# Second attention over whole 128-row blocks, with value rows placed by matmul and half-array score matmuls, in a one-core decoder layer

## The reference

```python
def proj(x, w):
    return (x @ w.T).reshape(B, -1, H, dk).transpose(0, 2, 1, 3)
Q, K, V = (proj(q, w_q), proj(k, w_k), proj(v, w_v))
scores = jnp.einsum('bhqd,bhkd->bhqk', Q, K) / jnp.sqrt(jnp.float32(dk))
scores = jnp.where(mask == 0, NEG, scores)
attn = jax.nn.softmax(scores, axis=-1)
out = jnp.einsum('bhqk,bhkd->bhqd', attn, V)
out = out.transpose(0, 2, 1, 3).reshape(B, S, D)
return out @ w_o.T
```

## Time and profile before

| | us |
|---|---|
| median of 3 runs | 1519.68 (1519.27 to 1520.58) |
| profiled execution | 1522.42 |
| its span | 1520.6 |
| PE busy | 1343.9 (88%) |
| DVE busy | 1113.7 (73%) |
| ACT busy | 925.7 (61%) |
| POOL busy | 730.0 (48%) |

### The profile page before, as it was taken

How to read it: one execution, slowest core, us unless ns; L and a number is a source line. 1 busy time by engine, 2 the same in 40 slices (tenths; PEclk the granted TensorE clock), 3 DMA queues, 4 the chain that set the end, 5 groups by cost and what they waited for, 6 DMA issues and landing times. The chain is left out here.

```text
span 1520.6 us, 48478 instructions
## 1 busy us (share of the span) xinstructions
PE 1343.9 (88%) x17429; PEld 1126.0 (74%) x17429; DVE 1113.7 (73%) x3110; ACT 925.7 (61%) x2255; POOL 730.0 (48%) x923
## 2 busy tenths in 40 slices
PE   3599989999999999999999999873899999999940
PEld 2478878888888888888888888641588888888820
DVE  4588878888888888888888889748455555555537
ACT  3566768777777777877777766623344444444426
POOL 3144564575575566566656644520244334444336
PEclk9799999999999999999999999995899999999975
DMA  9667666766757666666676664109532263323235
GB/s 219 127 155 162 164 149 164 143 137 179 143 132 186 138 143 162 155 145 143 167 146 135 156 112 88 26 15 411 165 79 74 77 157 98 76 77 76 74 134 208
DMA packets 293219, 209.01 MB, mean 137 GB/s; under 512 B 218782, under 2 KB 250654, under 8 KB 290560
## 3 DMA queue, kind: packets, MB, share of 16 engines
q1 hardware_dynamic: 281952, 184.01, 51.3%
q0 software_dynamic: 6816, 17.71, 3.9%
q10 hardware_dynamic: 4224, 4.19, 0.8%
HBM read 93.79 MB, written 65.93 MB: 105 GB/s over the span
## 5 line engine op out<-in xcount | busy, mean ns | idle before, releaser
L1635 PE MATMUL ps_e<-xt,wres 128*128 128x128 f16 x3408 | 343.4, 220 | 5.6 <-DMA xt<-xg 4.8
L1635 PEld LDWEIGHTS ps_e<-xt,wres 128*128 x3408 | 285.5, 98 | 77.6 <-issue 6.2
L1699 ACT ACTIVATE act_g<-ps_e,b 128x128 f32<-128x128 f32 x568 | 162.7, 369 | 207.8 <-PE ps_e L1635 207.6
L1642 PE MATMUL ps_e<-wres,g_hi 128*128 x568 | 214.5, 379 | 0.8 <-DVE g_lo L1722 0.8
L707 ACT ACTIVATE probs<-st_k,nmax 128x128 f32<-128x128 f32 (+1 forms) x512 | 199.6, 447 | 2.0 <-DVE nmax L914 1.9
L914 DVE CUSTOM_DVE_ANT_0 st_k<-ps,causal 128x128 f32<-128x128 f32 (+1 forms) x512 | 160.5, 351 | 35.6 <-PE ps L432 35.6
L1602 POOL DMA_INDIRECT z_scr<-e_y,dst_i x71 | 85.9, 1209 | 209.4 <-DVE e_y L1713 207.6
L714 ACT ACTIVATE pt_hi<-ps 128x384 f16<-128x384 f32 x256 | 125.0, 488 | 54.1 <-PE ps L440 31.8
L1644 PE MATMUL ps_e<-wres,g_lo 128*128 x568 | 154.8, 273 | 0.0
L1180 POOL TENSOR_TENSOR o_st<-o_norm,o_st 128x256 f16<-128x256 f32 x128 | 86.2, 673 | 133.6 <-ACT o_st L722 130.8
L1710 DVE SCALAR_TENSOR_TENSOR e_y<-ps_e,b 128x256 f32<-128x256 f32 x71 | 30.1, 424 | 158.9 <-PE ps_e L1644 158.9
(11 more groups left out here) (270 smaller groups left out, 4240.7 us busy)
## 6 DMA issues: line engine op xcount, KB each, us to landing
k_pair<-k_pair SPq DMA_DIRECT2D x96, 256.0 KB, 6.4
st_p<-in_moe_w SPq DMA_DIRECT2D x24, 768.0 KB, 6.2
w_scr<-st_p SPq DMA_DIRECT2D x24, 768.0 KB, 4.4
wres<-w_scr SPq DMA_DIRECT2D x18, 1024.0 KB, 21.6
v_scr<-v_tok SPq DMA_DIRECT2D x32, 512.0 KB, 3.8
v_pos<-v_scr SPq DMA_DIRECT2D x64, 256.0 KB, 6.2
q_st<-st_q SPq DMA_DIRECT2D x64, 128.0 KB, 3.4
z_scr<-zero SPq DMA_DIRECT2D x32, 256.0 KB, 3.6
```

The source lines that it names most:

```text
L1635: last = mm(out, w(c * FF + f * P, b, P), xt[:, t % X_BUFS, a, c], start=(m == 0), stop=(m == 5))
L1642: mm(out[:, 0:2 * D], g_hi[:, t % G_BUFS, f], w(KC * FF + f * D, 0, 2 * D), start=(f == 0), stop=False, skip_group_check=True)
L1699: nc.scalar.activation(act_g[:, k % 2, f], ps[:, 3 + 2 * (k % 2) + f // 4, (f % 4) * P:(f % 4 + 1) * P], ACT.Gelu, bias=bias[:, f:f + 1], ...
```

## The change

The 8 heads x 77 = 616 probabilities of a half are padded to 640 = 5 blocks of 128 (CHUNKS2) and are transposed and multiplied block by block, across the borders of heads. A block touches 2 or 3 heads; the 12 pairs of a block and a head are HEAD_SLOTS.

- Transposes: five of 128 x 128 in place of eight of 77. ACT and DVE write the parts from 128 x 384 and 128 x 256 in place of 77 x 512 twice.
- Values: for each block three matmuls over 128 rows with 34 or 51 columns (15 in place of 24). They need the values laid out by block rows with zeros outside each head (v2_own). In odd s, PE copies value rows to their block rows with a 0/1 matrix key_rows (value_rows, five matmuls for each cc), ACT brings them from PSUM to v2_rows (408 columns), and POOL multiplies by the 0/1 matrix slot_heads (own_values, 408 elements).
- Scores: k2_bd holds 4 heads. Heads 0 to 3 use rows 0 to 63 of the array and heads 4 to 7 rows 64 to 127, in alternation on two banks, six matmuls of 64 rows as before of 128. spread_k2 is half as wide.
- New waits: PE's value_rows waits for v2's low part, in the first pair for POOL's constants, and in its second half for ACT's first copy; x1's transposes wait for the second copy; pv2 waits for own_values. ACT's copy of the next values waits for value_rows.
- value_constants on POOL at the start of step 1 makes key_rows, slot_heads and the padding. head_rows is made in four selects in place of two.
- In the last norm a constant of 4 columns gives way to a broadcast of one.

The core of the diff:

```diff
@@ stage_c on PE
-                for j, bank in enumerate(banks2(t, cc)):
-                    out = bank[:, 0:4 * CTX]
-                    for m, (a, b) in enumerate(((q2_hi, 0), (q2_lo, 0), (q2_hi, 1))):
-                        last = mm(out, a[:, cc], k2_bd[:, b, cc, 4 * j:4 * j + 4].rearrange("p h k -> p (h k)"), start=(m == 0), stop=(m == 2))
+                for m, (a, b) in enumerate(((q2_hi, 0), (q2_lo, 0), (q2_hi, 1))):
+                    for j, bank in enumerate(banks2(t, cc)):
+                        rows = slice(j * P // 2, (j + 1) * P // 2)
+                        last = mm(bank[:, 0:4 * CTX], a[rows, cc], k2_bd[rows, b, cc].rearrange("p h k -> p (h k)"), start=(m == 0), stop=(m == 2))
...
-                    for n in range(4):
-                        last = nc.tensor.transpose(bank[0:CTX, n * P:(n + 1) * P], probs2_of(t, cc)[:, 4 * j + n], ident[:])
+                    for n, c in enumerate(BANK_CHUNKS[j]):
+                        last = nc.tensor.transpose(bank[:, n * P:(n + 1) * P], probs2_of(t, cc)[:, c * P:(c + 1) * P], ident[:])
@@ PE
+        def value_rows(t, cc):
+            if t % 2:
+                return
+            b = half(t)
+            if cc == 0:
+                pe.wait_ge(s_kv2_lo, 2 * (b + 1))
+                if t == 0:
+                    pe.wait_ge(s_const, N_SLOTS)
+            else:
+                pe.wait_ge(s_vrow_in, 2 * b + 1)
+            for c in range(CHUNKS2):
+                h, n, at = HB * cc + FIRST_HEAD[c], HEADS_IN[c], SLOT_AT[c] * 2 * (1 + DK)
+                last = mm(c6[:, at:at + n * 2 * (1 + DK)], key_rows[:, c * P:(c + 1) * P], v2[:, h:h + n].rearrange("p h k d -> p (h k d)"),
+                          start=True, stop=True)
+            last.then_inc(s_vrow, 1)
@@ pv2 on PE
+            if cc == 0 and even(t):
+                pe.wait_ge(s_vown, 2 * (half(t) + 1))
+            for c in range(CHUNKS2):
+                n, at = HEADS_IN[c], (HB * cc + FIRST_HEAD[c]) * (1 + DK)
+                out = c7[:, at:at + n * (1 + DK)]
+                v_hi, v_lo = (v2_own[:, cc, SLOT_AT[c]:SLOT_AT[c] + n, k] for k in range(2))
+                mm(out, high[:, c], v_hi, start=(c == 0), stop=False, skip_group_check=True)
+                mm(out, high[:, c], v_lo, start=False, stop=False, skip_group_check=True)
+                last = mm(out, low[:, c], v_hi, start=False, stop=(c == CHUNKS2 - 1), skip_group_check=True)
@@ step on PE
             if has(s):
                 pv(s, 0)
+            if has(s - 1):
+                value_rows(s - 1, 0)
             if has(s - 2):
                 stage_d(s - 2, 1)
             if has(s):
                 scores(s, 4)
                 turn_probs(s, 1)
+            if has(s - 1):
+                value_rows(s - 1, 1)
@@ ACT: behind piece(s - 4), and again behind pt(s, 1)
+            nc.scalar.activation(v2_rows[:, cc].rearrange("p s k d -> p (s k d)"), c6[:, 0:HEAD_SLOTS * 2 * (1 + DK)], ACT.Copy).then_inc(s_vrow_in, 1)
@@ POOL
+        def value_constants():
+            pool.wait_ge(s_lo, len(CHUNKS))
+            pool.wait_ge(s_const, N_MASK)
...
+        def own_values(t, cc):
+            if t % 2:
+                return
+            b = half(t)
+            pool.wait_ge(s_vrow_in, 2 * b + cc + 1)
+            if b >= 1:
+                pool.wait_ge(s_pv2, 2 * t)
+            nc.gpsimd.tensor_tensor(v2_own[:, cc].rearrange("p s k d -> p s (k d)"), v2_rows[:, cc].rearrange("p s k d -> p s (k d)"),
+                                    slot_heads[:].unsqueeze(2).to_broadcast([P, HEAD_SLOTS, 2 * (1 + DK)]), ALU.mult).then_inc(s_vown, 1)
@@ step on POOL
             if has(s - 1):
                 shift(s - 1, 0)
+                own_values(s - 1, 0)
             if has(s):
                 split_o(s, 1)
+            if has(s - 1):
+                own_values(s - 1, 1)
-        run(step, {-1: constants})
+        run(step, {-1: constants, 1: value_constants})
```

More of the change, by code:

```diff
@@ L25 @@
 HB = P // DK
+CHUNKS2 = (HB * CTX + P - 1) // P
+PADDED = CHUNKS2 * P
+FIRST_HEAD = [c * P // CTX for c in range(CHUNKS2)]
+HEADS_IN = [min(HB - 1, (c * P + P - 1) // CTX) - c * P // CTX + 1 for c in range(CHUNKS2)]
+SLOT_AT = [sum(HEADS_IN[:c]) for c in range(CHUNKS2)]
+HEAD_SLOTS = sum(HEADS_IN)
+BANK_CHUNKS = ((0, 1, 2), (3, 4))
 E = 8
@@ L498, in stage_c @@
                 if p == 0:
-                    pe.wait_ge(s_kv2_lo, 2 * (half(t) + 1))
+                    pe.wait_ge(s_vrow_in, 2 * (half(t) + 1))
                 for c in range(KC):
@@ L540, in pv2 @@
                 pe.wait_ge(s_lgc, t)
[L541 to L544, removed]
-                mm(c7[:, at:at + 1 + DK], high[:, n], v2_hi[:, h], start=True, stop=False, skip_group_check=True)
-                mm(c7[:, at + 1:at + 1 + DK], high[:, n], v2_lo[:, h], start=False, stop=False, skip_group_check=True)
-                last = mm(c7[:, at:at + 1 + DK], low[:, n], v2_hi[:, h], start=False, stop=True, skip_group_check=True)
+            if cc == 0 and even(t):
+                pe.wait_ge(s_vown, 2 * (half(t) + 1))
+            high, low = pt2_of(t, cc)
+            for c in range(CHUNKS2):
[5 more added lines that the diff above has]
+                last = mm(out, low[:, c], v_hi, start=False, stop=(c == CHUNKS2 - 1), skip_group_check=True)
             last.then_inc(s_pv2, 1)
@@ L1156, in constants @@
-            pool.wait_ge(s_const, N_CONST)
+            for n, rows in enumerate((slice(0, P // 2), slice(P // 2, P))):
+                pool.wait_ge(s_const, N_CONST - 4 + 2 * n)
+                nc.gpsimd.affine_select(out=head_rows[rows], in_=head_rows[rows], compare_op=ALU.is_ge, fill=0.0, base=0,
+                                        pattern=[[-DK, HB // 2], [0, CTX]], channel_multiplier=1).then_inc(s_const, 1)
+                pool.wait_ge(s_const, N_CONST - 3 + 2 * n)
+                nc.gpsimd.affine_select(out=head_rows[rows], in_=head_rows[rows], compare_op=ALU.is_ge, fill=0.0, base=DK - 1,
+                                        pattern=[[DK, HB // 2], [0, CTX]], channel_multiplier=-1).then_inc(s_const, 1)
@@ L1773, in final_block @@
     nmr = sb("f_nmr", [P, 2, Q], F32)
-    half4 = sb("f_half", [P, Q], F32)
+    half = keep["neg_half"]
     s_z = [sem("f_z%d" % n) for n in range(N)]
-    s_out, s_a, s_b, s_s, s_st, s_mv, s_ve, s_rstd, s_nmr, s_n, s_half = (
-        sem("f_" + n) for n in "out a b s st mv ve rstd nmr n half".split())
+    s_out, s_a, s_b, s_s, s_st, s_mv, s_ve, s_rstd, s_nmr, s_n = (
+        sem("f_" + n) for n in "out a b s st mv ve rstd nmr n".split())
     block = ctx.enter_context(nc.Block())
```

92 lines of the change are left out of this document (61 added, 31 removed).

## The result

The changed kernel took 1508.86 us, the median of four executions from 1507.96 to 1510.0. The kernel before took 1519.47 beside it. The ratio is 0.9931, 95% interval 0.9918 to 0.9944: faster by 0.7%. The forecast was 1523.0 in a range of 1513 to 1531, so both the side and the range were wrong. The profiled execution of the changed kernel took 1509.21 us with a span of 1507.5, 13.1 less than the span before.

A forecast was written before the change was run, and what follows sets the result against it. The prediction took POOL's queue from second norm to second transposes to set even steps, and odd ones beyond 1.07 us more. Terms 3.1 - 0.8 + 0.5 + 2.0 - 1.5 = +3.3 us gave 1523.0 us, range 1513 to 1531.

The forecast's parts named there:

- the spread costed at nothing: POOL's halved key spread lies where POOL waits for DVE: 0, at most 2.5 us gained in two steps.
- A: From the second transposes (L533) to the next step's projection (L494): -0.36 us in even and odd steps.
- B: From the projection (L494) to the second norm: +0.28 us in an odd step, 0 in an even one.
- C: From second norm to second transposes: 0 in even steps, +0.70 us in odd ones, past POOL's slack of 1.07 us.
- pair: An even and an odd step together: +0.26 us, twelve such pairs +3.1 us.
- The start: In step 1 PE waits for POOL's value_constants: +2.0 us, bounds 1.2 and 3.5; step 1 as an odd step: +0.5.
- The end: The last tile is one chain of shorter transposes, DVE parts and value matmuls: -1.5 us.
- Rival 2: PE is the bound after all: 1494 to 1470 us, or 1507 with half of the lower gain; chance 0.10.
- Rival 3: Switching the array's form for half-array scores costs PE time, half let through: 4.7 us, 1527.7 us; chance 0.12.
- Rivals 1 and 4: POOL's own_values cheap, 0.67 us apiece: 1515.9 us, chance 0.18; or dear, 1.24 apiece: 1532 us, chance 0.10.

The follow-up runs named there:

- before_pad32: The kernel before with one unused tile of 32 bytes a partition behind head_rows and nothing else; 1512.83 us, ratio 0.9957.
- half_padded: The kernel before with half-array score matmuls and the narrow key spread, both spread tiles keeping their old size; 1517.02 us, ratio 0.9977.
- half_scores: The kernel before with the six score matmuls on half the array and a key spread half as wide; 1512.81 us, ratio 0.9944.
- constants_early: The changed kernel with POOL's value_constants built ahead of the first key spread; 1505.29 us, ratio 0.9899 against the kernel before.
- full_spread: The kernel before with the score matmuls alone on half the array, the key spread as wide as before; 1519.25 us, ratio 1.0001.

## Why the prediction was wrong, step by step

**What failed first: nothing of the change was thought to reach the transfers.** No term of the sum covers the place of the tiles. The diff shows it, though: head_rows halves, and the tiles behind it move by 608 bytes, an odd multiple of 32. The move is worth 6.0 us alone (before_pad32), of some 8.9 that the start and step 4 gained in the first two records; part of the start's 3.7 is chance, since it ranges over 3 us in either group. The record of before also has a step 4 of 33.52 us beside steps of 28.80. I took its length as given and never asked what made it.

**What failed second: the spread costed at nothing.** The prediction named POOL's wait for DVE as cover. The cover is real for the start of the spread, but its end holds back DVE's first norm. Without the move of tiles the narrow spread is worth 3.0 us (half_padded): 0.12 in each odd step and 0.8 in step 1. The bound of 2.5 us for two steps contained it, but was not used.

**The steady steps, by terms** (a pair of steps, medians of steps 5 to 27):

| part | forecast | measured | what was mis-sized |
|---|---|---|---|
| A, both | -0.72 | -0.80 | close |
| B, odd | +0.28 | +0.25 | value rows 0.37, less 0.12 by the spread |
| B, even | 0 | +0.01 | |
| C, odd | +0.70 | +0.34 | see below |
| C, even | 0 | -0.14 | see below |
| pair | +0.26 | -0.36 | |

B came out right in part by luck. From the projection's first matmul to the second norm it is 9.03 us before, 8.92 in half_scores and 9.29 after. So the added work costs 0.37 and the narrow spread gives 0.12 back. The first norm starts 0.28 later in the step than before (9.30 and 9.02 us behind its start), as forecast. But it then falls beside the second spread instruction and is held by that one, odd step 15 after:

```profile
496.08 1.42 POOL L1290 TENSOR_TENSOR k_bd<-head_rows,k 128x308 f16<-128x308 f16 x2
496.73 0.92 DVE L1008 TENSOR_SCALAR x<-y,mv,rstd 128x256 f32<-128x256 f32 x1
```

It takes 0.92 us in place of 1.04, where 0.51 were enough in half_scores. No term of the prediction has this hold.

C is the term that turned the sign of the pair. own_values took 0.87 us, near the 0.90 of the line between two shapes:

```profile
L1246 POOL TENSOR_TENSOR st_xq<-st_xv,slot_heads 128x408 f16<-128x408 f16 x32 | 27.8, 870 | 0.0
```

The pair adds 1.66 us and not 1.75, since they follow at 0.83. The other part was in POOL's queue before, in both kinds of step (the last line is ACT's copy of o_norm, which the split reads):

```profile
512.99 0.67 POOL L1180 TENSOR_TENSOR o_st<-o_norm,o_st 128x256 f16<-128x256 f32 x1
513.62 3.40 POOL L1232 TENSOR_TENSOR st_p<-st_p 128x512 f16<-128x512 f32 x3
517.13 0.67 POOL L1180 TENSOR_TENSOR o_st<-o_norm,o_st 128x256 f16<-128x256 f32 x1
...
516.63 0.42 ACT L722 ACTIVATE o_st<-o_norm 128x256 f16<-128x256 f32 x1
```

Behind the three pieces, which end at 517.02, the split starts 0.11 late, where neighbours otherwise overlap by 0.04. In the changed kernel it starts at 511.20, before the pieces end at 511.24. So 0.15 us of waiting is gone. By the program the split waits for ACT's copy of o_norm and nothing else, and that copy ends at 517.05 before, 0.08 ahead of the split. In the changed kernel it ends at 510.04, while POOL is still busy with the pieces. In even step 14 the copy ends at 487.10 before, behind the pieces (487.08), and at 479.71 after, ahead of them (479.89). So the wait was for ACT, whose shorter copies stand ahead of this one; that it was them wasn't tested apart. This gives the even step its -0.14 and takes as much from the odd one. The prediction's "works without a gap" overlooked a gap of 0.11. Of 1.66 less 1.07 less 0.15, 0.44 is left, and 0.34 was measured. The 0.10 between them stays open.

Twelve pairs at -0.36 rather than +0.26 are 7.4 us, half of the miss. The single step is small, 0.6 us in 58, and the prediction had the size of each term to a few tenths. The twelvefold repetition made it decide.

**The start.** The forecast for step 1 was +2.5, and it measured +3.2. PE did wait for the constants, where and about as long as written (the prediction's items add up to 90.3, not 90.5):

```profile
87.22 0.47 PE L561 MATMUL ps<-v,st_xk 77*128 77x68 f16 x5 [2.34 <-POOL slot_heads L1234]
```

Without them ahead of the second half of the step, constants_early is 3.9 us shorter there. More than PE's wait is lost. POOL's reciprocal also stands behind the constants, without a gap (87.15 in the changed kernel), and the norm behind that.

**The end** was right in its sign: -1.5 forecast, -2.3 in the records shown. The other records of the kernel before have 527.5 to 527.7 us behind step 31, against 526.7 to 526.8 after, so 0.7 to 1.0 us of it is sure.

**The rivals.** Rival 2, PE the bound, is refuted by full_spread, although its figure for half of the lower gain, 1507, came nearest to the 1508.86. Rival 3 had one part right: the half-array groups pair. Three pairs take 0.50 where 0.40 would be three matmuls' spacing, so by this estimate the change of form costs about 0.1 us a group, not 0.3, and off the path. For the rule of the Trainium skill (TensorEngine Tiling (Array Packing), Key Properties), the independent tiles are confirmed, and a drain, if these 0.1 us are one, is short. Rivals 1 and 4 needed own_values at 0.67 or 1.24 and fell with 0.87. Rival 1 had the side right at 1515.9. Neither time was reached for the reason given with it.

## What to carry to other kernels

Before an edit that resizes a tile is costed, list which tiles behind it move and by how many bytes; the same copies of q_st took 2.8 or 3.4 us by 32 bytes of place here, and an unused tile tests it without touching the work. When an edit moves an operation out of a queue, check in the new trace that it has left the stretch that counts. Where one step of a repeated loop is longer than its neighbours in the trace (33.5 against 28.8), find its cause before forecasting a change, since the change may remove it by accident. An operation that is moved or narrowed on POOL is to be followed at its end as well as its start, because DVE may be held behind it.

## What the runs showed of the hardware

- Shifting the tiles by 32 bytes took 6.0 us off the time (ratio 0.9957), and shifting them by 64 bytes nothing (1.0005). q_st's packets of 128 bytes took 11.8 ns in place of 13.7, its copies of 128 KB landed 0.4 to 0.6 us sooner, and packets of 256 and 1024 bytes showed no such difference.
- Two half-array matmuls on different rows of the array and in different banks ran side by side: six of 308 columns in 0.50 us against 0.80.
- POOL's two-operand multiplication took 0.74 us for 308 elements, 0.87 for 408 and 1.28 for 616 at two bytes each, and its subtraction 1.22 for 616 at four. Two-byte operands were no cheaper.
- DVE's norm of 256 elements took 0.41 us alone and 0.51, 0.92 or 1.04 beside POOL's multiplications, ending 0.15 behind one of them each time.
